# A gated linear recurrence on one core: the table that orders TensorE's units within a body, and the steps at which the other engines' operations stand, written anew

## What is computed

```python
xa = _ln(x, ln1_w, ln1_b)
sx = jnp.concatenate([state[:, i0 + 1][:, None], xa[:, :-1]], axis=1) - xa
t = jnp.tanh((xa + sx * maa_x) @ maa_w1).reshape(B, L, 5, -1)
m = jnp.einsum('blfd,fdc->blfc', t, maa_w2)          # mw, mk, mv, mr, mg
xw = xa + sx * (maa_w + mw)                          # and xk, xv, xr, xg
w = jnp.exp(-jnp.exp(time_decay + jnp.tanh(xw @ decay_w1) @ decay_w2))
r, k, v, g = xr @ Wr.T, xk @ Wk.T, xv @ Wv.T, silu(xg @ Wg.T)
def step(s, inp):
    a = k_l[..., :, None] * v_l[..., None, :]
    out = jnp.einsum('bhs,bhst->bht', r_l, faaaa * a + s)
    return (a + w_l[..., None] * s, out)
y = group_norm(outs) * gn_w + gn_b
x = x + y * g @ Wo.T
xc = _ln(x, ln2_w, ln2_b)                            # shifted and mixed like xa
x = x + sigmoid(xr2 @ fWr.T) * (square(relu(xk2 @ fWk.T)) @ fWv.T)
```

## Time and profile before

| what | value |
|---|---|
| median of 3 runs | 4004.84 us |
| the profiled execution's own time | 4013.57 us |
| its span | 4011.8 us |
| TensorE busy | 3660.3 us (91%) |
| VectorE busy | 2950.0 us (74%) |
| ScalarE busy | 2034.6 us (51%) |
| GpSimd busy | 1832.1 us (46%) |
| bodies 1 to 13 of phase_c | 2440.97 to 3746.92 us |
| bodies 14, 15 and 16 | 3746.92 to 4011.8 us |

### The profile page before, as it was taken

How to read it: one execution, slowest core, us unless ns; L and a number is a source line. 1 busy time by engine, 2 the same in 40 slices (tenths; PEclk the granted TensorE clock), 3 DMA queues, 4 the chain that set the end, 5 groups by cost and what they waited for, 6 DMA issues and landing times. The chain is left out here.

```text
span 4011.8 us, 71126 instructions
## 1 busy us (share of the span) xinstructions
PE 3660.3 (91%) x21676; PEld 2802.5 (70%) x21676; DVE 2950.0 (74%) x6738; ACT 2034.6 (51%) x5166; POOL 1832.1 (46%) x1256
## 2 busy tenths in 40 slices
PE   7999999899999988999999878999999999999976
PEld 6777777777777767999999655555555656565543
DVE  6777777888888876555665457787877888787783
ACT  5777777777777775545555322333332333333321
POOL 5444444644444440000000036676766767676661
PEclk9999999999999999999999988999999999999988
DMA  5344434544444442001000300000000000000000
GB/s 151 94 105 114 108 96 100 145 123 122 126 110 115 117 121 98 32 31 47 31 31 31 121 14 19 25 25 25 25 25 25 25 25 25 25 25 25 19 19 16
DMA packets 143809, 256.54 MB, mean 64 GB/s; under 512 B 24384, under 2 KB 29248, under 8 KB 142624
## 3 DMA queue, kind: packets, MB, share of 16 engines
q1 hardware_dynamic: 143648, 254.48, 23.3%
HBM read 107.61 MB, written 33.55 MB: 35 GB/s over the span
## 5 line engine op out<-in xcount | busy, mean ns | idle before, releaser
L463 POOL TENSOR_TENSOR a_prob<-a_prob,a_rsums 128x512 f32<-128x512 f32 x512 | 542.4, 1061 | 780.2 <-DVE a_rsums L645 780.0
L1443 POOL TENSOR_TENSOR c_S<-c_S,c_rT 128x1024 f32<-128x1024 f32 x256 | 604.6, 2362 | 311.3 <-DVE c_S L1798 311.3
L535 ACT ACTIVATE a_prob<-a_t,a_tmin 128x256 f32<-128x256 f32 x1024 | 512.7, 501 | 364.3 <-DVE a_tmin L638 363.3
L1798 DVE TENSOR_TENSOR_SCAN c_S<-c_wT,c_vb 128x512 f32<-128x512 f32 x512 | 625.2, 1221 | 50.5 <-issue 8.4
L1793 DVE TENSOR_TENSOR c_vb<-c_kT,c_vb 128x510 f32<-128x510 f32 x512 | 351.4, 686 | 282.2 <-PE c_vb L2007 256.8
L634 DVE SCALAR_TENSOR_TENSOR a_ps_s<-a_ps_s,a_mask 128x512 f32<-128x512 f32 x512 | 357.4, 698 | 172.6 <-PE a_ps_s L741 103.4
L638 DVE CUSTOM_DVE_ANT_0 a_t<-a_ps_s,a_mneg 128x256 f32<-128x256 f32 x1024 | 394.2, 422 | 60.1 <-issue 0.7
L751 PE MATMUL a_ps_t<-w_ident,a_prob 128*128 128x128 f32 x2048 | 323.4, 281 | 27.9 <-ACT a_probT L545 18.6
L2007 PE MATMUL c_vb<-c_vhl,c_spread 128*128 128x512 f32 x512 | 275.0, 563 | 63.5 <-DVE c_S L1798 50.3
L741 PE MATMUL a_ps_s<-a_stack 96*128 96x256 f32 x1024 | 230.7, 308 | 84.4 <-DMA a_stack<-a_parts_qk 65.1
L545 ACT COPY a_probT<-a_ps_t 128x512 f32<-128x512 f32 x512 | 288.5, 564 | 1.6 <-PE a_ps_t L751 1.6
(11 more groups left out here) (255 smaller groups left out, 10027.9 us busy)
## 6 DMA issues: line engine op xcount, KB each, us to landing
a_stack<-a_parts_qk SPq DMA_DIRECT2D x768, 128.0 KB, 2.4
x<-w_x_out SPq DMA_DIRECT2D x48, 512.0 KB, 2.8
w_x_in<-x SPq DMA_DIRECT2D x48, 512.0 KB, 3.9
w_x_out<-x SPq DMA_DIRECT2D x32, 512.0 KB, 3.5
w_x_in<-in_x SPq DMA_DIRECT2D x16, 512.0 KB, 3.6
w_x_out<-in_x SPq DMA_DIRECT2D x16, 512.0 KB, 3.6
a_enc<-in_ctx SPq DMA_DIRECT2D x16, 512.0 KB, 4.4
b_xb<-x SPq DMA_DIRECT2D x16, 512.0 KB, 4.4
```

Source lines behind the costliest of these rows:

```text
L463: nc.gpsimd.tensor_tensor(prob[:, h % 4, :, :], prob[:, h % 4, :, :], rsums[:, h, :].unsqueeze(2).to_broadcast([P, TC, T]), ALU.mult).then ...
L535: op = nc.scalar.activation(prob[:, n % 4, tc, :], t[:, n % 2, tc, :], ACT.Exp, bias=tmin[:, n, tc:tc + 1], scale=-1.0, accum_out=psums[:, ...
L1443: nc.gpsimd.tensor_tensor(S[:, n % 4, :, :], S[:, n % 4, :, :], rT[:, par, :, :], ALU.mult).then_inc(z_ready, 1)
L1798: nc.vector.tensor_tensor_scan(flat(pair(S[:, n % 4, :, :], i)), flat(pair(wT[:, par, :, :], i)), flat(x), 0.0, ALU.mult, ALU.add).then_in ...
```

## The change

Only numbers change, and one rule for them. FILLS gets another order: mr0 and mv0 go from the end of n = 3 behind zT at n = 4, and zT and they now stand between the broadcasts (4,0) and (4,1), with mr1 and mv1 behind (4,1); o0 keeps its place. r0 and r1 both stand at the end of n = 6; mg0 and dec20 follow at n = 7 ahead of broadcast (7,1); bonus0 stands ahead of broadcast (8,1), bonus1 and xcT behind it. kk0, kk1, rr0, rr1 (before kk0, rr0, kk1, rr1) spread over n = 11 to 13, and rr1 goes behind xaT. On GpSimd add_xa's steps for k, r, v, g go from 0, 5, 5, 9 to 1, 3, 4, 10, ln1_root from 10 to 11 and add_r from 9 to 10; on ScalarE ln2_norm goes from 8 to 7, scale_k and scale_r from 9 and 10 to 10 and 11, and ln1_norm from 12 to 11. FILLS_0, the table of body 0, changes only in its n = 12 and 13 (kk1 ahead of rr0, and rr1 behind xaT, all units that body 0 leaves out), and LN1_AT_0 gives body 0 its old step for ln1_norm. Every operation, shape and buffer count stays.

```diff
-    FILLS = {0: (["mw0", "mk0"], ["mw1", "mk1"]), 1: (["g0"], ["y0", "y1"]), 2: (["g1", "dec1"], []), 3: (["k0"], ["k1", "mr0", "mv0"]), 4: ([], ["zT0", "zT1"]), 5: (["mr1", "mv1"], ["o0"]), 6: (["o1"], ["r0"]), 7: ([], ["r1", "mg0", "dec20"]), 8: ([], ["bonus0", "bonus1", "xcT0", "xcT1"]), 9: (["mg1", "dec21"], ["v0"]), 10: ([], ["v1"]), 11: (["kk0"], ["rr0", "kk1"]), 12: ([], ["rr1"]), 13: (["xaT0", "xaT1"], []), 14: (["kv0"], ["kv1"]), 15: ([], ["t"])}
+    FILLS = {0: (["mw0", "mk0"], ["mw1", "mk1"]), 1: (["g0"], ["y0", "y1"]), 2: (["g1", "dec1"], []), 3: (["k0"], ["k1"]), 4: (["zT0", "zT1", "mr0", "mv0"], ["mr1", "mv1"]), 5: ([], ["o0"]), 6: (["o1"], ["r0", "r1"]), 7: (["mg0", "dec20"], []), 8: (["bonus0"], ["bonus1", "xcT0", "xcT1"]), 9: (["mg1", "dec21"], ["v0"]), 10: ([], ["v1"]), 11: (["kk0"], []), 12: (["kk1"], ["rr0"]), 13: (["xaT0", "xaT1"], ["rr1"]), 14: (["kv0"], ["kv1"]), 15: ([], ["t"])}
...
-    AT = {"y": 1, "variance": 2, "root": 2, "norm": 2, "gate": 3, "ln2_root": 6, "ln2_norm": 8, "sxc": 8, "scale_k": 9, "scale_r": 10, "add_k": 9, "add_r": 9, "out": 15, "ln1_stats": 11, "ln1_root": 10, "ln1_norm": 12, "sx": 12, "scale_x": 14, "add_x": 13, "rk": 6}
-    ADD_XA = (0, 0, 5, 5, 9)
+    AT = {"y": 1, "variance": 2, "root": 2, "norm": 2, "gate": 3, "ln2_root": 6, "ln2_norm": 7, "sxc": 8, "scale_k": 10, "scale_r": 11, "add_k": 9, "add_r": 10, "out": 15, "ln1_stats": 11, "ln1_root": 11, "ln1_norm": 11, "sx": 12, "scale_x": 14, "add_x": 13, "rk": 6}
+    ADD_XA = (0, 1, 3, 4, 10)
...
+    LN1_AT_0 = {"ln1_stats": 11, "ln1_root": 11, "ln1_norm": 12}
...
-            return LN1_AT[name] if name in LN1_AT and isinstance(k, int) and k == -1 else AT[name]
+            if name in LN1_AT and before(k, 1):
+                return (LN1_AT if before(k, 0) else LN1_AT_0)[name]
+            return AT[name]
```

More of the change, by code:

```diff
@@ L1104, in phase_c @@
-    FILLS_0 = {0: ([], ["Xt"]), 1: (["g0"], ["mw0", "mk0"]), 2: (["mw1", "mk1"], ["g1"]), 3: ([], ["dec1", "k0"]), 4: ([], ["k1"]), 5: ([], ["mr0", "mv0"]), 6: (["mr1", "mv1"], []), 7: ([], ["r0"]), 8: ([], ["r1"]), 9: (["y0", "y1"], ["v0"]), 10: (["bonus0"], ["bonus1", "mg0", "dec20"]), 11: (["v1"], ["mg1", "dec21"]), 12: (["zT1", "o0", "o1"], ["xcT0", "xcT1", "kk0", "rr0", "kk1", "rr1"]), 13: (["xaT0", "xaT1"], []), 14: (["kv0"], ["kv1"]), 15: ([], ["t"])}
-    AT = {"y": 1, "variance": 2, "root": 2, "norm": 2, "gate": 3, "ln2_root": 6, "ln2_norm": 8, "sxc": 8, "scale_k": 9, "scale_r": 10, "add_k": 9, "add_r": 9, "out": 15, "ln1_stats": 11, "ln1_root": 10, "ln1_norm": 12, "sx": 12, "scale_x": 14, "add_x": 13, "rk": 6}
@@ L1107, in phase_c @@
-    ADD_XA = (0, 0, 5, 5, 9)
+    FILLS = {0: (["mw0", "mk0"], ["mw1", "mk1"]), 1: (["g0"], ["y0", "y1"]), 2: (["g1", "dec1"], []), 3: (["k0"], ["k1"]), 4: (["zT0", "zT1", "mr0", "mv0"], ["mr1", "mv1"]), 5: ([], ["o0"]), 6: (["o1"], ["r0", "r1"]), 7: (["mg0", "dec20"], []), 8: (["bonus0"], ["bonus1", "xcT0", "xcT1"]), 9: (["mg1", "dec21"], ["v0"]), 10: ([], ["v1"]), 11: (["kk0"], []), 12: (["kk1"], ["rr0"]), 13: (["xaT0", "xaT1"], ["rr1"]), 14: (["kv0"], ["kv1"]), 15: ([], ["t"])}
+    FILLS_0 = {0: ([], ["Xt"]), 1: (["g0"], ["mw0", "mk0"]), 2: (["mw1", "mk1"], ["g1"]), 3: ([], ["dec1", "k0"]), 4: ([], ["k1"]), 5: ([], ["mr0", "mv0"]), 6: (["mr1", "mv1"], []), 7: ([], ["r0"]), 8: ([], ["r1"]), 9: (["y0", "y1"], ["v0"]), 10: (["bonus0"], ["bonus1", "mg0", "dec20"]), 11: (["v1"], ["mg1", "dec21"]), 12: (["zT1", "o0", "o1"], ["xcT0", "xcT1", "kk0", "kk1", "rr0"]), 13: (["xaT0", "xaT1"], ["rr1"]), 14: (["kv0"], ["kv1"]), 15: ([], ["t"])}
@@ L1126, in phase_c @@
     units, units_0 = table(FILLS), table(FILLS_0)
-    TAIL = ["xaT0", "xaT1", "kv0", "kv1", "t"]
+    TAIL = ["xaT0", "xaT1", "rr1", "kv0", "kv1", "t"]
     for u in (units, units_0):
```

## The result

The change makes the kernel faster: 3983.57 us in the median of 5 runs (3982.39 to 3986.14) against 4004.38 us of the kernel before, measured beside it (3997.45 to 4007.41). The ratio is 0.9944, with a 95% interval of 0.9931 to 0.9957. That is 20.8 us, or 0.6%. The forecast was 3980 us, 24.6 us less than before, with a range of 3950 to 4006.

What follows compares the result with a forecast made beforehand. TensorE was taken to bound the kernel. Per body 3.8 - 1.25 - 0.85 = 1.7 us, 22.1 in 13 bodies, plus 2.5 in body 14, made 24.6; from 4004.84 that gave 3980 us, range 3950 to 4006.

Steps and rivals of the forecast that it cites:

- TensorE bounds the bodies, and its idle time is what an order can win: Bodies 1 to 13: TensorE busy 1232.49 of 1305.95 us, so 73.5 us idle, 5.6 per body, could be won.
- n = 4 and 5: Around broadcasts (4,0) to (5,1): both scan waits, 1.69 us, go; a 0.25 wait of mr1 for zT's buffers comes.
- The gate and o0, r0: o0's gate is ready with 0.5 us in hand; r's sum ends before r0, so r0's 0.63 wait goes.
- bonus0 and (8,1): bonus0 still waits 0.4 of 1.48 us for r*k; broadcast (8,1) waits 0.6 for scan (7,1).
- kk, rr and xaT, 0.85: At n = 11 to 13, xaT and rr1 wait for ScalarE's ln1_norm: 0.85 us per body, upper bound 2.66.
- The sum per body, 1.7: Net gain per body: 3.8 us of old waits less 1.25 and 0.85 of remaining and new ones; 22.1 in 13 bodies.
- The clock, left as it was: TensorE's granted clock, costed as unchanged, with busy time in the 13 bodies staying near 1232 us.
- The rival that filled waits give clock back: Stretches at 1.2 GHz go with the waits: at most 31 us more, 3949 us; chance 0.15.
- t's tanh: Wait for the tanh of t, ahead of the next body's first mixes, stays at 1.56 us per body.
- Bodies 14 to 16: Body 14, which has no ln1, gains 2.5 us; bodies 15 and 16 gain nothing.
- GpSimd's backlog: Seven GpSimd operations in a row pass delays to bonus0, so the 13 bodies gain nothing: 4004 us; chance 0.18.
- The slower case, ScalarE blocked by ln1_norm: At n = 11, reads of kk0 and kk1 queue behind ln1_norm: 21 us slower, 4026 us; chance 0.12.

Runs made afterwards that it cites:

- front_addxa5: front_only with GpSimd's sums of xa for r and v put back behind read-out 5 (add_xa at 0, 1, 5, 5, 9); 4023.59 us, ratio 1.0033 to before.
- scal_after: The kernel of the change with the two small 128x2 operations ending the ln1 and ln2 statistics moved from VectorE to GpSimd; 3986.08 us, ratio 0.9947 to before.
- back_only: The kernel before with only the change's order and steps from n = 9 on (kk, rr, xaT, ln1); 4013.88 us, ratio 1.0013.
- kv1_behind_t: The kernel of the change with kv1 moved behind t, so its matmuls cover the tanh of t; 3982.81 us, ratio 0.9934 to before.
- kv1_steps: kv1_behind_t with the other engines' steps from n = 9 on put back as in the kernel before; 3979.68 us, ratio 0.9927 to before.
- scal_before: The kernel before with the two small 128x2 operations ending the ln1 and ln2 statistics moved from VectorE to GpSimd; 4013.01 us, ratio 1.0015.
- front_only: The kernel before with only the change's order for n = 0 to 8, add_xa at 0, 1, 3, 4, 9 and ln2_norm at 7; 3972.59 us, ratio 0.9913.

## Why the prediction came out right, point by point

**TensorE bounds the bodies, and its idle time is what an order can win.** Right: the change took 27.4 us of idle time out of 73.5 and left the work as it was.

**n = 4 and 5.** Both scan waits (1.69) went. mr1 was to wait 0.25 for zT's buffers; it waited 0.09 in body 12, and the waits view has only one such wait, of 0.2, in the 13 bodies. Right.

**The gate and o0, r0.** Free, as worked out. GpSimd's sum for r waits 3.41 us for VectorE ahead of read-out 4 in body 12 and nothing behind it comes too late but r*k. `front_addxa5` shows the price of its old place, 2.57 per body at r0.

**bonus0 and (8,1).** Worked out 0.4 and 0.6; measured 0.54, 0.28 and, at (9,0), where none was expected, 0.38. Together 1.2 against 1.0. The name of the releaser, ScalarE's decay operation in some bodies, is that of the operation that ended last; it lies within the same few tenths as r*k, as `scal_after` shows, where r*k alone is named.

**kk, rr and xaT, 0.85.** The size was near (0.65), the mechanism was not the one that acted. I had it that xaT and rr1 would wait for ln1_norm on ScalarE. What acted was VectorE, held in an operation of 128x2 elements while GpSimd ran read-out 11. I had costed VectorE's end of the statistics as in the trace before, without asking what GpSimd would now be doing beside it. The working itself held both times, statistics ready at 3619.1 and read-out 11 up to 3620.9, so that they overlapped; the trace before had ln2's addition at 0.75 us beside a read-out. The waits that I named were there behind it: `scal_after` brought them out with 0.73 per body. That 0.85 came near 0.65 is luck.

**The sum per body, 1.7.** In idle time it was 2.1 (27.4 in 13, against 22.1 worked out). Higher busy time then took 0.7 of it. The two errors, 5.3 us more of idle time won and 9.6 us more of busy time, stand against each other, so that the total came nearer than its terms.

**The clock, left as it was.** That is the term that was off, and the sign that I had named for it (TensorE busy far from 1232) is there in part. Busy time rose by 9.6 us in the 13 bodies. Single bodies: two of 13 had PEclk 1.00 before, none has more than 0.98 after. The rival that filled waits give clock back fell: of the runs, `back_only` with the most idle time (80.7 us) had 1232.86 busy, the change with 46.1 had 1242.11. Where the clock falls, body 13 of the change shows:

```profile
3629.38 1.15 PE L1965 MATMUL c_ps<-c_tT,c_mix 33*128 33x256 f32 x8 [1.73 <-ACT c_tT L1548]
3631.19 2.08 PE L1965 MATMUL c_ps<-c_tT,c_mix 33*128 33x256 f32 x8
```

Behind the wait for the tanh the first pair of mixes takes 1.15 us, the second 2.08; from 3631 to 3637 the granted clock is 0.50, which is 1.2 GHz. With that wait covered (`kv1_behind_t`) busy time was 1215.43 and six bodies had PEclk 1.00; of the five with the wait of 4.6 to 5.4 us none had. `kv1_steps` had 1216.73. That goes together with the wait, but is not a proof of it: the same edit also put kv1's matmuls between t and the mixes. How much of the 9.6 us is the change's own stays open. The granted clock of the executions of before is 0.957 to 0.963 and its profiled one stands at the lower end; the five of the change have 0.957 to 0.960 (mean 0.9584 against 0.9603), and `scal_before`, with an edit off TensorE's path, has 0.9587. So some of the loss is there in the mean too, but an edit that leaves TensorE's waits nearly as they were makes as much.

**t's tanh.** Stayed: 20.3 and 20.2 us.

**Bodies 14 to 16.** 2.5 us were forecast, all in body 14. That body went from 101.81 to 97.06 us; its idle time fell by 2.9, near the forecast, and its busy time by 1.9, which is clock (PEclk 0.95 and 0.96; in `scal_before`, with the order of before, 1.00 and a body of 97.3 us). Bodies 15 and 16, costed at nothing, were 2.5 shorter, 1.6 of it busy time.

**The rivals.** GpSimd's backlog did not give the waits back: r*k ended within 0.5 us of where I had it. The slower case, ScalarE blocked by ln1_norm, did not come: ScalarE stood 9.95 us at that place in body 12, and no wait of TensorE for it appears.

## What to carry to other kernels

Before moving work in a table of this kind, take each wait by itself and write down who is late next, on every engine, in the units of the trace; the waits that came of it here were worked out to within 0.4 us, one of them by another mechanism. A change that moves many steps should be tried in halves: here one half carried all of the gain and the other took some 11 us of it back (7 in idle time of bodies 1 to 13), so that `front_only` at 3972.59 us has the lowest median and ratio of the kernels run, though the interval of its ratio overlaps with that of `kv1_steps`. And when the operations of two engines slide against each other, look for small operations that come to run beside a large one, and for the same pair elsewhere in the trace before.

## What the hardware showed that I had not expected

A VectorE operation on 128x2 elements in SBUF (tensor_scalar, or tensor_tensor with both inputs in SBUF) took 0.16 to 0.17 us with GpSimd idle, and up to 2.08 us when GpSimd had a 128x1024 operation in hand, ending with it. In the 26 of the change's 13 bodies it cost VectorE 45 us, in the 26 of before 8. The products and scans of the same kernel did not stretch (685 and 1220 ns in the mean after, 686 and 1221 before); the product reads one of its inputs in PSUM.

TensorE's busy time for the same work followed the place of one wait and not the sum of its waits. Without the 1.6 us ahead of the mixes, matmuls that use 33 rows, TensorE was busy 1215 and 1217 us in the 13 bodies, with 70.3 and 71.5 us idle; the kernels that have that wait were busy 1232 to 1248 us, with 39.1 to 80.7 idle. That the wait is the cause is argued, not shown.

At each further turn of the loop VectorE stood some 2 us (1.9 to 2.3 before and in the change) ahead of its first product for nothing that the profile shows. Before and in the change at most 1.0 us of a body came of it, since TensorE waited there for the tanh; once that wait was covered it showed as 4.6 to 5.4 us, five times.
